# A graph-and-attention layer on one core: the front's node embedding by column part, turned edge counts in two bank sets, and the attention-score weights partly on PE

## The reference

```python
xn = _layernorm(x, axis=-1)                       # x: (1250, 768)
x1 = relu(xn @ W_ah + b_ah)
def gat_conv(x, src, dst, W, a_src, a_dst, b):    # three of them, on x1; 4 heads of 192
    h = (x @ W).reshape(N, H, C)
    as_n = (h * a_src).sum(-1)
    ad_n = (h * a_dst).sum(-1)
    e = leaky_relu(as_n[src] + ad_n[dst], 0.2)
    m = segment_max(e, dst)
    p = exp(e - m[dst])
    alpha = p / segment_sum(p, dst)[dst]
    out = segment_sum(alpha[:, :, None] * h[src], dst)
```

## Time and profile before

| | |
|---|---|
| median of 3 runs | 1605.49 us (1596.41 to 1607.78) |
| profiled execution, its own time | 1602.74 us |
| its span | 1600.4 us |
| busy, share of the span | PE 89%, DVE 68%, ACT 29%, POOL 2% |
| first product of the embedding | 46.36 us |
| first one-hot product | 131.07 us |
| first product of the next block | 318.73 us |

### The profile page before, as it was taken

One profiled execution on the slowest core, in us unless ns is written; L12 is line 12 of the kernel. 1 busy time (PEld: TensorE's weight loads), 2 busy tenths in 40 slices (PEclk: granted clock), 3 DMA queues, 4 the chain that ended last, 5 costly groups with the idle time before them and its releaser, 6 DMA issues.

```text
span 1600.4 us, 24066 instructions
## 1 busy us (share of the span) xinstructions
PE 1417.4 (89%) x9522; PEld 1353.7 (85%) x9523; DVE 1087.8 (68%) x2046; ACT 469.9 (29%) x779; POOL 39.6 (2%) x42
## 2 busy tenths in 40 slices
PE   3877887799999969678899999999999999998788
PEld 2877877598888869668799999999999999997654
DVE  7779877378888863226677667757767676766644
ACT  3220011323333341123343243243334324322231
POOL 0110000000000004000000000000000000000000
PEclk9997989999999989879899999999999999999995
DMA  6330000012222038511001101012011010005003
GB/s 201 109 119 0 0 0 0 11 70 79 79 79 79 17 109 253 183 41 43 20 33 35 63 33 35 1 62 67 0 62 38 31 62 33 6 1 142 1 0 96
DMA packets 23440, 91.71 MB, mean 57 GB/s; under 512 B 3437, under 2 KB 4688, under 8 KB 20285
## 3 DMA queue, kind: packets, MB, share of 16 engines
q1 hardware_dynamic: 21857, 86.66, 16.5%
q10 hardware_dynamic: 1500, 3.88, 0.8%
HBM read 79.46 MB, written 11.06 MB: 57 GB/s over the span
## 4 chain that ended last, share of the span: by engine, by line
PE 48%; DVE 7%; ACT 3%; issue 1%; DVEq 0%
PE psum L1417 20%; PE psum L101 8%; PE psum L102 8%; PE psum L103 8%; DVE prob L1145 2%; PE psum L1500 2%; DVE prob L1139 2%; DVE hN L1159 1%; ACT prob L1293 1%; PE psum L1431 1%; DVE x1l L1165 1%; PE psum L1468 1%; PE psum L1480 0%; ACT x1h L1299 0%; DVE acc L1180 0%
## 5 line engine op out<-in xcount | busy, mean ns | idle before, releaser
L1417 PE MATMUL psum<-hN,prob 125*125 125x193 f32 x2400 | 413.1, 329 | 12.4 <-DVE hN L1159 7.6
L1417 PEld LDWEIGHTS psum<-hN,prob 125*125 125x125 f32 x2400 | 398.3, 189 | 14.0 <-issue 10.9
L1293 ACT ACTIVATE prob<-prob,acol 125x1250 f32<-125x1250 f32 x120 | 161.0, 1342 | 398.2 <-DVE prob L1139 398.2
L1145 DVE SCALAR_TENSOR_TENSOR prob<-prob,cnt 125x1250 f32<-125x1250 f32 x120 | 174.8, 1457 | 80.3 <-ACT prob L1293 80.3
L1139 DVE SCALAR_TENSOR_TENSOR prob<-vrow,ncol,urow 125x1250 f32<-125x1250 f32 x120 | 181.9, 1516 | 0.0
L636 DVE CUSTOM_DVE_ANT_0 junk<-mask,arow 125x1250 bf16<-125x1250 uint8 x120 | 174.8, 1457 | 3.1
L101 PE MATMUL psum<-wph,x1h 128*125 128x384 f32 x360 | 134.3, 373 | 26.7 <-DVE x1l L1165 26.7
L508 PEld LDWEIGHTS psum<-hot_dst,hot_src 125*125 125x125 bf16 x1960 | 125.5, 147 | 27.3 <-DVE hot_src L387 27.3
L508 PE MATMUL psum<-hot_dst,hot_src 125*125 125x125 bf16 x1960 | 126.8, 232 | 23.6 <-DVE hot_src L387 23.6
L101 PE MATMUL psum<-woh,xlh 128*125 128x384 f32 x360 | 127.8, 355 | 15.7 <-DVE acc L1180 15.7
L102 PE MATMUL psum<-wpl,x1h 128*125 128x384 f32 x360 | 126.3, 351 | 0.0
(11 more groups left out here) (199 smaller groups left out, 2196.8 us busy)
## 6 DMA issues: line engine op xcount, KB each, us to landing
arow<-scratch_a SPq DMA_DIRECT2D x12, 625.0 KB, 3.9
urow<-scratch_uv SPq DMA_DIRECT2D x12, 625.0 KB, 4.1
vrow<-scratch_uv SPq DMA_DIRECT2D x12, 625.0 KB, 5.6
wl<-in_w_gat SPq DMA_DIRECT2D x6, 1152.0 KB, 8.0
wq_raw<-in_w_qkv SPq DMA_DIRECT2D x6, 1152.0 KB, 6.6
wp_raw<-in_w_pair SPq DMA_DIRECT2D x6, 1152.0 KB, 7.5
wo_raw<-in_w_out SPq DMA_DIRECT2D x6, 1152.0 KB, 5.1
xN<-in_x SPq DMA_DIRECT2D x10, 336.0 KB
```

Of the source, the lines that this page charges most:

```text
L1145: nc.vector.scalar_tensor_tensor(prob[n % RING][:, :], prob[n % RING][:, :], 1.0, cnt[:, n % NT, :], op0=ALU.min, op1=ALU.mult).then_inc(p ...
L1293: nc.scalar.activation(prob[n % RING][:, :], prob[n % RING][:, :], ACT.Exp, bias=acol[:, n // NT, n % NT:n % NT + 1]).then_inc(e_ready, 1)
L1417: last = nc.tensor.matmul(bank(t // 2)[0:P, 193 * (t % 2):193 * (t % 2) + 193], ring[:, t * P:(t + 1) * P], hN[i % 2][:, j, 193 * s:193 * ...
```

## The change

- **x1T by column part, between the transposes.** The 18 groups now run column part by column part (`X1`), with all six weight tiles kept in SBUF (`w_high`, `w_low`, 6 each). PE turns four tiles, then alternates a group of the first column part with the transposes of one further tile. The weights come in SP's queue between the x tiles; `half_layer(0)`, `half_layer(1)` come behind them and behind the two small transfers of `ends`.
- **node_id and eye.** POOL makes `node_i` first and then a 125x2375 bf16 `eye` (zeros with an identity in it) at the very start; DVE waits for both and makes `node_id` before its first statistics.
- **wa shared.** DVE makes the columns of two convolutions (96 entries), PE those of the third: 36 products of a turned weight tile with 8 columns (`w_turned`, 2.36 MB, and `a_block`), which ACT copies into `wa`.
- **Scores first.** The score products and their transposes stand ahead of the counts; the lowest score is taken by DVE after window 0's one-hot tiles.
- **Counts turned.** The stationary operand is `hot_dst`, the moving one `hot_src` in three parts of 418, 416 and 416, so a window's counts stand with the destination on the partition. Windows alternate between banks 0 to 2 and 3 to 5. A product with `eye` starts each window (the self loops). ACT copies the window to SBUF (`ct`), DVE makes that window's `mask` rows from it, and PE turns `ct` with ten f32 transposes one window later, through banks 6 and 7, from which ACT writes `cnt`. The 100 transposes of `some` and `mask`'s copies go.
- **wq_low** (the low part of the next block's first weights) is subtracted by DVE behind the last window's one-hot tiles, and no longer by POOL.

```diff
+        ROWS = 2
+        X1 = tuple((c, o) for c in range(len(CH)) for o in range(KT))
+        XL = (8, 14, 2 * NT)
+        TURNS = ((6, 0, 4), (7, 4, 4), (6, 8, 2))
+
+        def at_window(w, c):
+            return bank(3 * (w % 2) + c)
...
+            own.done(nc.gpsimd.memset(eye[:, :], 0.0))
+            nc.gpsimd.tensor_copy(eye[:, N - P:N], ident[0:P, 0:P]).then_inc(const_ready, 1)
...
+            dve.wait_ge(const_ready, 5)
+            own.done(nc.vector.tensor_copy(node_id[:, :], node_i[:, :]))
...
-            for layer in range(LAYERS):
+            for layer in range(ROWS):
...
+            def has_edge(w):
+                dve.wait_ge(ct_ready, 3 * (w + 1))
+                nc.vector.tensor_scalar(mask[:, w, :], ct[w % 2][:, :], 1.0, None, ALU.min).then_inc(mask_ready, 1)
...
+                if w == 0:
+                    lowest()
+                else:
+                    has_edge(w - 1)
+            dve.wait_ge(wq_ready, 1)
+            nc.vector.tensor_tensor(g["wq_low"][:, :, :], g["wq_raw"][:, :, :], g["wq_high"][:, :, :].bitcast(F32),
+                                    ALU.subtract).then_inc(wq_ready, 1)
+            has_edge(NT - 1)
...
+            for t in range(4):
+                turn_x(t)
+            for i in range(len(X1)):
+                hidden(i)
+                if i + 4 < NT:
+                    turn_x(i + 4)
+
+            pe.wait_ge(wT_in, 32)
+            for k in range(KT):
+                for c in range(KT):
+                    last = nc.tensor.matmul(bank(7)[:, 2 * HL * k:2 * HL * (k + 1)], wT[:, c, 128 * k:128 * (k + 1)],
+                                            a_blk[:, c, :], start=c == 0, stop=c == KT - 1)
...
+            def turn_count(w):
+                pe.wait_ge(ct_ready, 3 * (w + 1))
+                if w == 0:
+                    pe.wait_ge(ab_taken, 1)
+                for k, (at_bank, t0, n) in enumerate(TURNS):
+                    if len(TURNS) * w + k >= 2:
+                        pe.wait_ge(turn_free, len(TURNS) * w + k - 1)
+                    for t in range(n):
+                        last = nc.tensor.transpose(bank(at_bank)[0:P, P * t:P * (t + 1)], ct[w % 2][:, (t0 + t) * P:(t0 + t + 1) * P],
+                                                   ident[0:P, 0:P])
+                    last.then_inc(turn_full, 1)
...
+            for w in range(NT):
+                if w >= 2:
+                    pe.wait_ge(ct_ready, 3 * (w - 1))
+                for c, (c0, n) in enumerate(CH):
+                    e0 = N - P - w * P + c0
+                    last = nc.tensor.matmul(at_window(w, c)[0:P, 0:n], eye[:, N - P:N], eye[:, e0:e0 + n], start=True,
+                                            stop=False, skip_group_check=True)
...
+                        for c, (c0, n) in enumerate(CH):
+                            last = nc.tensor.matmul(at_window(w, c)[0:P, 0:n], hot_dst[:, e, 0:P], hot_src[:, e, c0:c0 + n],
+                                                    start=False, stop=False, skip_group_check=True)
+                        last.then_inc(hot_free, 1)
+                nc.tensor.matmul(at_window(w, 0)[0:P, 0:1], eye[:, 0:P], eye[:, 0:1], start=False, stop=True,
+                                 skip_group_check=True).then_inc(ct_full, 1)
+                if w:
+                    turn_count(w - 1)
+            turn_count(NT - 1)
```

More of the change, by code:

```diff
@@ L181, in front @@
         prod = at("prod", MASK_AT + 4096, [128, C])
[L183 to L189, removed]
@@ L457, in _ @@
                 nc.scalar.activation(abT[:, c0:c0 + n], bank(4 + i)[0:2 * HEADS, 0:n], ACT.Copy).then_inc(at_ready, 1)
-            for i in range(2 * NT):
-                j, half = i // 2, i % 2
-                act.wait_ge(some_full, i + 1)
-                nc.scalar.activation(mask[:, 5 * half:5 * half + 5, j * P:(j + 1) * P],
-                                     bank(3 + i % 4)[0:P, :].bitcast(BF16)[:, 0:640].rearrange("p (t n) -> p t n", n=128)[:, :, 0:P],
-                                     ACT.Copy).then_inc(some_free, 1)
+            act.wait_ge(wq_in, 16)
@@ L468, in _ @@
-            for i in range(2 * NT):
-                t, half = i // 2, i % 2
-                if not half:
-                    pe.wait_ge(xn_ready, t + 1)
-                if i >= 4:
-                    pe.wait_ge(xl_ready, i - 3)
-                for k in range(3):
-                    f = 3 * half + k
-                    last = nc.tensor.transpose(bank(i % 4)[:, k * P:(k + 1) * P], xN[:, t, f * 128:(f + 1) * 128],
-                                               ident[0:P, 0:P])
-                last.then_inc(xt_full, 1)
@@ L479, in _, with turn_x @@
-            pe.wait_ge(xl_ready, 2 * NT)
-            for i in range(KT * 3):
-                o, (c0, n) = i // 3, CH[i % 3]
-                if i % 3 == 0:
+            def turn_x(t):
+                pe.wait_ge(xn_ready, t + 1)
+                for i in (2 * t, 2 * t + 1):
+                    if i >= 4:
+                        pe.wait_ge(xl_ready, i - 3)
+                    for k in range(3):
+                        f = 3 * (i % 2) + k
+                        last = nc.tensor.transpose(bank(i % 4)[:, k * P:(k + 1) * P], xN[:, t, f * 128:(f + 1) * 128],
+                                                   ident[0:P, 0:P])
+                    last.then_inc(xt_full, 1)
@@ L1544 @@
     qkv = a["L0_mix_W_qkv"].T.reshape(KT, 128, 3, PAIRS, 128).transpose(3, 1, 0, 2, 4).reshape(PAIRS, 128, KT, 384)
+    spread = np.zeros((HL, C, 2, HL), np.float32)
+    for h in range(HL):
+        spread[h, :, 0, h], spread[h, :, 1, h] = a["L0_gnn_a_src2"][h], a["L0_gnn_a_dst2"][h]
     data = {
```

290 lines of the change are left out of this document (150 added, 140 removed).

## The result

The changed kernel takes 1557.49 us (median of 4 runs, 1554.69 to 1558.87), the kernel before 1604.45 us (4 runs, 1596.41 to 1607.78): a ratio of 0.9708, 95% interval 0.9684 to 0.9731. I had said 1568 with a range of 1555 to 1586. The time lies in the range, but where rival B stood (1555 to 1560: the clock stays up), and under the 1560 at which the main case began.

What follows compares the result with a forecast made beforehand. Only the front changes, its bounding engine differing by stretch, neither PE nor DVE full in the counts. Gains 8.9 + 3 + 21.4 + 2.3 = 35.6 us take 1602.74 to 1567, by the median 1570; forecast 1568, range 1555 to 1586.

Steps and rivals of the forecast that it cites:

- rival B: Counts: the clock stays up, low-clock episodes vanish, 8 us less; 1560, or 1555 with turning better hidden; chance 0.14.
- the main case: Whole front as forecast term by term: 1568 us, 1560 to 1577; chance 0.57.
- Start: Front's start and embedding: statistics near 6.6 us, first group near 26, embedding's end near 97 in place of 110.4.
- The 1 us for POOL's subtractions: Embedding: POOL's six subtractions fall among DVE's normalising, at most six times 1.5 us, mostly in slack; 1 us added.
- DVE's part of wa: After x: DVE free near 57, reach 5.7 us, 96 entries 38.4, one wait 4.6; end 105.7 in place of 127.
- PE's part of wa: After the embedding: 36 products take 4 to 9 us from 97, done by 106, hidden by DVE; uncovered up to 1 us.
- Scores: Ahead of the counts: 12.8 + 0.6 + 1.3 + 1.76 us, first unit at 122.2, 8.9 earlier than 131.07.
- Counts: The ten windows: sum 146 us plus 8 for the low clock kept in gaps, 154 against 157, 3 us gained.
- Rival C: Counts: windows cost more, by exposed weight loads (17 us) or low clock after every gap (20); 1583 to 1588; chance 0.16.
- Rivals D and E: D: interleaved start saves nothing, 1593 to 1600, chance 0.08. E: PE at 1.2 GHz through the counts, 1652, chance 0.05.
- Tail and block end: After the last unit: 5.3 us in place of 26.7, 21.4 gained; block end 3.75 to some 1.4, 2.3 gained.

Runs made afterwards that it cites:

- Experiment 5: Changed kernel with PE's part of wa operand-swapped, 12 wide products (384 columns moving) instead of 36: 1554.9 us, ratio 0.97.
- Experiment 2: Kernel before, with twenty unused identity products ahead of PE's wait for ACT's copies in each window: 1598.03 us, ratio 0.9974.
- experiment 1: Changed kernel with all windows in one set of banks (0 to 2) instead of two: 1586.76 us, ratio 0.9908.
- experiment 9: Changed kernel again, 1558.21 us; with the changes of experiment 5 and experiment 6 together, 1549.12; with scores also behind the counts, 1547.06.
- experiment 6: Changed kernel with DVE making node_id without waiting for eye, and ACT splitting weight tiles ahead of its x copies: 1555.27 us, ratio 0.9715.

## Why the prediction was right, and where it was not

*Start: right.* Statistics near 6.6, measured 6.24; the first group near 26, measured 25.00, in steps of 0.35 us to 30.7 and of 0.19 behind; the embedding's end near 97, measured 94.99. The six transposes took 0.80 to 0.86 us. The 1 us for POOL's subtractions was the right size for PE (four waits of 0.26 to 0.29), though DVE lost 6.4 us to them (four times 1.6). The Trainium skill (SBUF — State Buffer, "Who interferes with whom") had only the normalising exposed and the low parts free, and the trace agrees with both: the normalising shows 2.29 in place of 0.68, and the one pair of low parts that lay beside POOL takes 0.95 us, as long as a pair without it (10.48 in the kernel before).

```profile
19.96 1.80 POOL L310 TENSOR_TENSOR wah_low<-wah_raw,wah_high 128x768 fp32r<-128x768 f32 x1 [14.60 <-ACT wah_high L444]
20.42 0.95 DVE L332 TENSOR_TENSOR xnl<-psum,xnh 128x375 fp32r<-128x375 f32 x2
```

The section frees a DVE instruction with at most one SBUF input only "outside the 2-port perf modes", a condition that my sentence on it left out.

*DVE's part of wa: 4.8 us earlier than forecast.* It ended at 100.9, not 105.7. DVE was free of x at 55.4 instead of 57, and the reach took 2.6 us, not 5.7: the figure that I had taken from the earlier trace rows held two small instructions of 1.8 and 1.7 us, beside POOL's subtraction (44.41, 3.58 us), that take 0.17 and 0.23 in the changed kernel, where no POOL work lies beside them. I had named that lengthening and not taken it out of this term.

*PE's part of wa: wrong, 5.8 us on the path.* The failed step is "PE's 36 products of 8 columns lie between 0.12 ... and 0.25 each ..., so 4 to 9 us from 97: done by 106, hidden by DVE". They took 11.71 us, and 10.7 to 13.1 in the other executions. The price of one was inside my bounds at full clock, 0.22 us, though by luck: each product is two instructions in the trace (x72), as the score rows of before said already (x36 for the 18 products of L517), and I had priced one, from transposes. What the term lacked is the clock, which fell to 0.50 at 99 and made it 0.43: 3.7 us, and without them the products end at 103. As it was they end at 106.70, DVE at 100.9, so they, not DVE, set when the scores start; DVE's early end makes up the rest of the 5.8 us.

*Scores: 12.8 us forecast, 15.5 measured,* since they began on the low clock that those products left (0.50 to 112.6). Experiment 5 has both at 1.00 and 12.75. Together with 1.05 us less to the first unit (0.71 from the first product with `eye`, where I had kept 1.76) this gives 125.07 for 122.2.

*Counts: 142.3 against 154.* The failed step is the one where I chose: "PE's gap is as long as before, so I keep it: 8 us". The windows by themselves were to take 146; they took 142.3, the 3.7 being 0.46 a gap (3.0 instead of 3.46, again the 1.76 before the first unit, which was 1.28) in eight gaps. The other 8 are the low clock, which is gone from windows 2 to 9. That is rival B, to which I had given 0.14 against the main case's 0.57. I had held the length of PE's pause against rival B, but what counted was whether PE did anything in it: before, it waited 1.53 us of the gap for ACT and 1.01 to 1.06 for DVE; now the turning stands where the first wait stood, and the longest idle piece is 0.5 to 0.7. Experiment 2 shows this in the old kernel, experiment 1 the reverse in the new one. It isn't the whole story of the clock: it fell at window 0's start in five traces without such an idle piece (experiment 9). The steps were otherwise right: window 0 31.4 (31.0), window 1 22.0 (22), 20 units 14.5 (14.8), 0.56 a unit on PE (0.57), PE as the pace at 12 units.

*Rival C, not borne out.* Neither the weight loads show (0.56 a unit) nor is the clock low after the gaps. The Trainium skill (TensorE: Matmul & The Clock Gate, "Part 4: PE-mode transpose") would have a transpose count for less than a product; here the ten transposes and three products of a gap left the clock at 1.00 (178.45 to 181.45). A gap with transposes alone isn't among these runs, but a longer stretch is: behind the counts PE turns `some` with 100 bf16 transposes. In the kernel before the clock stayed at 1.00 through all of them (302.84 to 313.4). In experiment 2 it fell to 0.50 among them and was back at 1.00 before they ended, with nothing but such transposes on PE:

```profile
297.20:300.70 3.50, 3.50 (x32) 3.45 (x33) 1.45 (x3) 3.50 (x7) 0.00 (x0) 0.53 0.00 0
300.70:306.00 5.30, 4.50 (x49) 3.38 (x49) 3.42 (x6) 5.30 (x11) 0.00 (x0) 1.00 0.01 2
```

So transposes alone did bring the full clock back, which speaks against the page's sentence that it doesn't engage for them; whether one counts for less than a product stays open. The agreement that I saw in the first stretch of the kernel before proves little: PE was idle for more than half of it, and for 3.28 us right before 46.36.

*Rivals D and E: not seen.* Groups of 4.57 us with transposes between them, and no long stretch at 1.2 GHz.

*Tail and block end: right,* at 21.0 and 2.3. `wq_low` took 2.55 us on DVE ("under 3") and lay beside the turning of window 8 (267.21 to 269.76).

The forecast of 1568 was 10.5 us above the result: 12 us too many in the counts, less 3 in their start, and the rest in what varies between executions. That the time fell inside the range is luck in part: the range was drawn wide enough for B, and the errors had opposite signs, which kept the forecast closer than its steps were.

## What to carry to other kernels

Before you price a gap by its length, see what the engine does in it: work moved into a wait can pay twice, by itself and by the clock of what follows, and a second set of banks is worth more than the wait that it removes. Count instructions in the trace, not calls in the program, wherever a product's operands are plain f32. And when something is moved ahead "because it is ready", try it behind as well: where one engine is full from end to end, its order gains only what a neighbour's wait costs.

## What the runs showed of the hardware that I had not expected

- PE was busy for all of 94.99 to 106.70 with products of 8 columns, and its granted clock fell from 1.00 to 0.50 at 99; with the operands swapped, 384 columns moving, it stayed at 1.00 through the same work. So a PE that reads as fully busy is no sign of a full clock.
- 1.35 us of useless products in a gap kept the clock up in windows 3 to 6 and saved 7.5 us (experiment 2).
- A product of plain f32 operands stands as two instructions: 0.66 us for 384 columns (7.91 for 12) at a granted 1.00; with 8 moving columns and 128 stationary ones 0.22 us at 1.00 and 0.43 at 0.50.
- One kernel's clock differs between executions: the changed kernel's fell at window 1's start in one trace (17.95 us) and not in the other (17.39), behind the same wait of 3.5 us.
- The third x tile had come by 10.0 us in one execution and came at 11.9 in another (experiment 6), a spread larger than the 1.5 us won ahead of it.
